# The affine step of a layer norm moved from ScalarE to VectorE in a transformer layer on eight cores

## The chip, the cores and the metric

The kernel runs on the 8 cores of one Trainium2 chip. All cores run the same program, each on its own 1024 tokens. The metric is the device time of the slowest core in microseconds. TensorE is called PE here, VectorE DVE, ScalarE ACT, GpSimd POOL and SyncE SP, as the profile calls them.

## What is computed

One layer: a gated linear attention with its own layer norm, a residual and a layer norm, a gated feed-forward network of inner width 8192, again a residual and a layer norm. Inputs are 4 x 2048 tokens of width 2048 in f32. The part that the change touches is the layer norm on `y`, its gate, and the product with `Wo` that follows:

```python
q = (x @ Wq).reshape(B, S, H, Dh)
v = (x @ Wv).reshape(B, S, H, Dh)
# states: new = sigmoid(beta) * prev + v_t, along the tokens
y = (q * states).reshape(B, S, D)
mu = jnp.mean(y, axis=-1, keepdims=True)
var = jnp.var(y, axis=-1, keepdims=True)
y = (y - mu) * jax.lax.rsqrt(var + LN_EPS) * ln_g + ln_b
gate = jax.nn.silu(x @ Wg)
y = y * gate
return y @ Wo
...
x = _layernorm(x + attention(x))
h = jax.nn.silu(x @ w_gate.T) * (x @ w_up.T)
x = _layernorm(x + h @ w_down.T)
```

## The kernel before, in words

The program is written by hand for each engine: every block (`@blk.vector`, `@blk.scalar`, ...) appends its instructions to the queue of one engine, in the order of the Python code, and engines wait for each other on counting semaphores. `tick` lets an instruction raise its engine's semaphore (sT, sV, sS, sP for PE, DVE, ACT, POOL) and returns the count; `mil` keeps such counts by name, and `wait_ge(sX, n)` holds an engine's queue until engine X has reached n. An engine also waits for itself in this way, where one of its instructions reads what the one before it has written: `v.wait_ge(sV, cnt["V"])`. Nothing reorders the queues.

Stages, in order: load and transpose x (`tbuf`, features in partitions, 16 tiles of 128 x 1024 tokens); q projection into `qbuf`; carry-in state; v projection into `vbuf`; scan over 8 chunks of tokens with the gate projection between the chunks, its Silu going to `bbuf`; sums for the layer norm on `y` (L698 squares on DVE, L710 and L714 column sums on PE); the row statistics on one partition (L734 to L756); a broadcast of them over 128 partitions by PE into four PSUM banks (L764, L765): `p[n2]` holds 1/std and `p[2+n2]` holds -mu/std of the 512 tokens of half n2.

Then comes the loop around the change (L774 to L816). It runs over n2 (two halves of 512 tokens) and over the 16 feature tiles dt, 32 turns in all. A turn takes one 128x512 tile of `qbuf` and does, on DVE, `tmp = y * p[n2]` (L790) and `tmp = tmp + p[2+n2]` (L793); on ACT, `tmp2 = Identity(tmp * ln_g + ln_b)` with both as per-partition operands from `lngb` (L801); on DVE, `y = tmp2 * gate` (L811), bf16, back into `qbuf`. `tmp` and `tmp2` are f32 views of the two halves of the bf16 scratch tile `sqscr`. There is one `tmp` and one `tmp2`, so turns don't overlap, but for the first instruction of a turn, which may start as soon as ACT is done with the turn before.

The `Wo` product follows (L958 to L1006): for each half of the `wo` panels, each of 8 chunks of 128 tokens and each of 4 panels, PE accumulates 16 matmuls over the feature tiles (L981) in bank 4 or 5 in turn. Each of the 16 waits for its tile's turn of the loop (`mil[("y2", gk)]`, L980). The bank is freed by a cast on DVE (L995). All casts stand in DVE's queue behind all 32 turns. The `wo` panels come by DMA from POOL's queue (L266, from L956 and L964), and SP loads x for the residual (L831). After that DVE and ACT do the layer norm (L841 to L902), PE transposes (L927), and the feed-forward network runs in 64 pairs of gate and up products (L1090, L1121) with the down product (L1184) between them.

Of the kernel before, what the change touches and what calls it, by code (L numbers as in the profile page):

```python
# [7 lines left out]
F32 = mybir.dt.float32  # L8
BF16 = mybir.dt.bfloat16
AF = mybir.ActivationFunctionType  # L10
ALU = mybir.AluOpType
# [27 lines left out]
def build_program(c: Cfg):  # L39
    nc = bass.Bass("TRN2", target_bir_lowering=False)  # L40
    D, TOK, INTER = c.D, c.TOK, c.INTER
    H, KT, NCH, NT, NN2 = c.H, c.KT, c.NCH, c.NT, c.NN2
# [33 lines left out]
    qbuf = sbuf("qbuf", [128, KT * TOK], BF16)  # L76
# [15 lines left out]
    lngb = sbuf("lngb", [128, 2 * KT], F32)  # L92
# [5 lines left out]
    sqscr = sbuf("sqscr", [128, max(2 * TOK, D, 4 * NT)], BF16)  # L98
# [6 lines left out]
    p = [psum(f"p{i}", [128, 512], F32) for i in range(7)]  # L105
# [7 lines left out]
    sT, sV, sS, sP = sem("sT"), sem("sV"), sem("sS"), sem("sP")  # L113
    cnt = {"T": 0, "V": 0, "S": 0, "P": 0}
    semmap = {"T": sT, "V": sV, "S": sS, "P": sP}

    def tick(inst, e, k=1):
        inst.then_inc(semmap[e], k)
        cnt[e] += k
        return cnt[e]  # L120
# [6 lines left out]
    def dtick(inst, name):  # L127
        ds[name][1] += 16
        inst.then_inc(ds[name][0], 16)
        return (name, ds[name][1])  # L130
# [17 lines left out]
    blk = es.enter_context(nc.Block())  # L148
    mil = {}
# [16 lines left out]
    @blk.sync  # L166
    def _(sy):
        dtick(sy.dma_start(llrow[:1, :H], beta16), "small")
        dtick(sy.dma_start(llrow[:1, H:H + 1], cflag), "small")
        dtick(sy.dma_start(lngb[:, 0:KT], lng_col), "small")  # L170
        mil["small_in"] = dtick(sy.dma_start(lngb[:, KT:2 * KT], lnb_col),
                                "small")
# [176 lines left out]
    for pi in range(NPAN):  # L349
# [6 lines left out]
        for dtl in range(NDT):  # L356
            dt = pi * NDT + dtl
# [412 lines left out]
    mil["l1bc_done"] = cnt["T"]  # L770

    first_y2 = [True]
    prev_y2 = [None]
    for n2 in range(NN2):  # L774
        for pi in range(NPAN):
            for dtl in range(NDT):
                dt = pi * NDT + dtl
                ggrp = pi * NDT * NN2 + dtl * NN2 + n2

                @blk.vector  # L780
                def _(v, dt=dt, n2=n2, ggrp=ggrp):
                    if first_y2[0]:
                        first_y2[0] = False
                        v.wait_ge(sT, mil["l1bc_done"])
                    v.wait_ge(sS, mil[("gsil", ggrp)])
                    if prev_y2[0] is not None:
                        v.wait_ge(sS, mil[("y2t3", prev_y2[0])])
                    ysl = qbuf[:, dt * TOK + n2 * NT: dt * TOK + (n2 + 1) * NT]
                    tmp = sqscr[:, 0:2 * NT].bitcast(F32)
                    tick(v.tensor_mul(tmp, ysl, p[n2][:, 0:NT]), "V")  # L790
                    v.wait_ge(sV, cnt["V"])
                    mil[("y2t2", ggrp)] = tick(
                        v.tensor_add(tmp, tmp, p[2 + n2][:, 0:NT]), "V")  # L793

                @blk.scalar
                def _(sc, dt=dt, n2=n2, ggrp=ggrp):
                    sc.wait_ge(sV, mil[("y2t2", ggrp)])
                    tmp = sqscr[:, 0:2 * NT].bitcast(F32)
                    tmp2 = sqscr[:, 2 * NT:4 * NT].bitcast(F32)
                    mil[("y2t3", ggrp)] = tick(  # L800
                        sc.activation(tmp2, tmp, AF.Identity,  # L801
                                      bias=lngb[:, KT + dt:KT + dt + 1],
                                      scale=lngb[:, dt:dt + 1]), "S")

                @blk.vector
                def _(v, dt=dt, n2=n2, ggrp=ggrp):
                    v.wait_ge(sS, mil[("y2t3", ggrp)])
                    ysl = qbuf[:, dt * TOK + n2 * NT: dt * TOK + (n2 + 1) * NT]
                    tmp2 = sqscr[:, 2 * NT:4 * NT].bitcast(F32)
                    gsl = bbuf[:, dt * TOK + n2 * NT: dt * TOK + (n2 + 1) * NT]  # L810
                    inst = v.tensor_mul(ysl, tmp2, gsl)  # L811
                    mil[("y2", ggrp)] = tick(inst, "V")
                prev_y2[0] = ggrp
                if n2 == NN2 - 1:
                    mil[("y2dt", dt)] = cnt["V"]
        mil[("y2h", n2)] = cnt["V"]  # L816
# [490 lines left out]
def _get_nc(cfg):  # L1307
    key = (cfg.D, cfg.TOK, cfg.INTER, cfg.WINP)
    if key not in _NC_CACHE:
        _NC_CACHE[key] = build_program(cfg)  # L1310
    return _NC_CACHE[key]
# [66 lines left out]
```

## Time and profile before

| | |
|---|---|
| runs shown | 2313.89 and 2378.39 us, median 2346.14 us |
| profiled execution, its own time | 2313.54 us |
| its span, slowest core (core 5) | 2311.9 us |
| spans of the eight cores | 2302.1 to 2311.9 us |
| PE busy | 1921.7 us, 83% of the span |
| DVE busy | 557.8 us, 24% |
| ACT busy | 410.1 us, 18% |
| POOL busy | 110.2 us, 5% |

The profiled execution is one run, and its span is the time from the first to the last instruction of the slowest core. A busy time is the sum over the whole span. A low share says nothing about a stage: an engine can be idle for most of the span and still be what others wait for in one stage of it. Rows are read with start times in us from the start of the span, and a bracket at the end of a row gives the idle time of the engine before that instruction and who ended it.

### The profile page before, as it was taken

What the parts mean: (1) busy time and instruction counts of PE and PEld (TensorE: products, weight loads), DVE (VectorE), ACT (ScalarE), POOL (GpSimd) and SP (SyncE); (2) the same over time, 40 slices, a digit from 0 to 9 for tenths busy, and PEclk for the clock granted to TensorE, in tenths of its full rate; (3) what the DMA queues carried; (4) which work ended last, traced back from release to release, by engine and by line L of the source; (5) the groups of instructions that cost most, each with busy time, mean ns of one, the idle gap of its engine ahead of it and who ended that gap; (6) DMA issues with size and microseconds to landing.
All of it is one profiled execution on the core that took longest, in us unless ns stands there. A gap on an engine that the chain in (4) does not pass through costs nothing.

```text
span 2311.9 us, 25430 instructions; the slowest of 8 cores (2302.1 to 2311.9 us)
## 1 busy us (share of the span) xinstructions
PE 1921.7 (83%) x9898; PEld 970.9 (42%) x9898; DVE 557.8 (24%) x1319; ACT 410.1 (18%) x466; POOL 110.2 (5%) x230
## 2 busy tenths in 40 slices
PE   4898999811196639999999999999999999997760
PEld 2347864300164424444444444444444444443320
DVE  4222234644413450010111101111111111111154
ACT  0100015334300102222121121121112112110002
POOL 1000000000000000000000000000000000000000
PEclk9999999955597759999999999999999999999885
DMA  8652343420005105335453354353444334423113
GB/s 122 115 91 37 58 72 72 71 59 0 0 11 104 70 2 90 73 73 96 86 92 73 55 94 84 57 95 73 74 73 91 74 55 91 77 43 64 37 37 145
DMA packets 32452, 161.03 MB, mean 70 GB/s; under 512 B 3668, under 2 KB 3668, under 8 KB 22100
## 3 DMA queue, kind: packets, MB, share of 16 engines
q0 software_dynamic: 29744, 142.62, 34.6%
q1 hardware_dynamic: 2596, 16.79, 1.9%
q8 instruction: 85, 1.39, 0.2%
q14 instruction: 27, 0.22, 0.0%
HBM read 293.62 MB, written 8.39 MB: 131 GB/s over the span
## 4 chain that ended last, share of the span: by engine, by line
PE 78%; DVE 8%; DMA 5%; ACT 5%; issue 4%; DVEq 0%; POOL 0%; ACTq 0%; POOLq 0%; SPq 0%
PE p L1090 19%; PE p L1121 19%; PE p L1184 18%; PE p L981 5%; PE p L492 5%; PE p L590 5%; PE p L370 4%; DMA warena<-wd_t 2%; ACT L801 2%; DMA bbuf<-x_loc 1%; ACT sqscr L801 1%; DVE sqscr L793 1%; DVE sqscr L790 1%; DMA warena<-wo 1%; DVE mscr L1025 1%
## 5 line engine op out<-in xcount | busy, mean ns | idle before, releaser
L1090 PE MATMUL p<-tbuf,warena 128*128 128x512 bf16 x2048 | 465.0, 380 | 7.4 <-DMA warena<-wgu_t 7.4
L1121 PE MATMUL p<-tbuf,warena 128*128 128x512 bf16 x2048 | 462.9, 379 | 0.0
L1108 ACT ACT_TABLE_LOAD x128 | 164.2, 1283 | 1015.5 <-PE p L1090 1015.5
L1090 PEld LDWEIGHTS p<-tbuf,warena 128*128 128x128 bf16 x2048 | 200.8, 98 | 250.6 <-issue 10.4
L981 PE MATMUL p<-warena,qbuf 128*128 128x256 bf16 x1024 | 155.1, 304 | 177.8 <-DVE bbuf L995 101.1
L1121 PEld LDWEIGHTS p<-tbuf,warena 128*128 128x128 bf16 x2048 | 200.3, 98 | 241.7
L1184 PE MATMUL p<-warena,vbuf 128*128 128x512 bf16 x1024 | 232.1, 389 | 42.0 <-DMA warena<-wd_t 34.2
L1184 PE MATMUL p<-warena,qbuf 128*128 128x512 bf16 x1024 | 222.3, 379 | 0.0
L981 PEld LDWEIGHTS p<-warena,qbuf 128*128 128x128 bf16 x1024 | 109.6, 107 | 224.6 <-issue 188.1
L1200 DVE TENSOR_TENSOR bbuf<-bbuf,p 128x512 bf16<-128x512 bf16 x128 | 88.0, 687 | 378.9 <-PE p L1184 378.9
L1184 PEld LDWEIGHTS p<-warena,vbuf 128*128 128x128 bf16 x1024 | 101.2, 100 | 172.3 <-issue 58.4
L1184 PEld LDWEIGHTS p<-warena,qbuf 128*128 128x128 bf16 x1024 | 100.2, 98 | 120.8
L1141 DVE TENSOR_TENSOR qbuf<-sscr,p 128x512 bf16<-128x512 f32 x64 | 44.0, 688 | 407.6 <-PE p L1121 407.6
L1141 DVE TENSOR_TENSOR vbuf<-sscr,p 128x512 bf16<-128x512 f32 x64 | 44.0, 688 | 398.2 <-PE p L1121 398.2
L370 PE MATMUL p<-tbuf,warena 128*128 128x512 bf16 x512 | 114.5, 388 | 10.6 <-DVE qbuf L384 8.5
L590 PE MATMUL p<-tbuf,warena 128*128 128x512 bf16 x512 | 114.8, 383 | 0.0
L1050 POOL DMA_DIRECT2D warena<-wgu_t x128 | 67.6, 533 | 970.0 <-PE p L1121 798.0
L492 PE MATMUL p<-warena,tbuf 128*128 128x256 bf16 x1024 | 113.5, 273 | 0.0
L492 PEld LDWEIGHTS p<-warena,tbuf 128*128 128x128 bf16 x1024 | 99.7, 98 | 13.5 <-issue 2.0
L606 ACT ACT_TABLE_LOAD x32 | 41.1, 1283 | 311.6 <-PE p L590 311.6
L370 PEld LDWEIGHTS p<-tbuf,warena 128*128 128x128 bf16 x512 | 50.9, 100 | 73.9 <-issue 16.2
L1108 ACT ACTIVATE sscr<-p 128x512 f32<-128x512 f32 x128 | 76.4, 597 | 1.4
(126 smaller groups left out, 780.9 us busy)
## 6 DMA issues: line engine op xcount, KB each, us to landing
warena<-wgu_t POOLq DMA_DIRECT2D x128, 512.0 KB, 6.9
warena<-wd_t POOLq DMA_DIRECT2D x32, 1024.0 KB, 13.3
warena<-wq POOLq DMA_DIRECT2D x8, 1024.0 KB, 9.4
warena<-wv POOLq DMA_DIRECT2D x8, 1024.0 KB, 9.9
warena<-wg POOLq DMA_DIRECT2D x8, 1024.0 KB, 8.9
warena<-wo POOLq DMA_DIRECT2D x8, 1024.0 KB, 18.5
sscr<-x_loc SPq DMA_DIRECT2D x8, 1024.0 KB, 4.8
out_loc<-sscr SPq DMA_DIRECT2D x8, 1024.0 KB, 4.1
```

What stands on the lines that cost most here:

```text
L370: inst = t.matmul(p[bk][:, 0:NT], warena[:, slot * WSL + k * PW + dtl * 128: slot * WSL + k * PW + (dtl + 1) * 128], tbuf[:, k * TOK + n2 ...
L492: inst = t.matmul(p[bk][:, 0:PW], tbuf[:, k * TOK + ci * 128: k * TOK + (ci + 1) * 128], warena[:, slot * WSL + k * PW: slot * WSL + (k + ...
L590: inst = t.matmul(p[bk][:, 0:NT], warena[:, slot * WSL + k * PW + dtl * 128: slot * WSL + k * PW + (dtl + 1) * 128], tbuf[:, k * TOK + n2 ...
L801: sc.activation(tmp2, tmp, AF.Identity, bias=lngb[:, KT + dt:KT + dt + 1], scale=lngb[:, dt:dt + 1]), "S")
L981: inst = t.matmul(p[bk][:, 0:PW], qbuf[:, k * TOK + ci * 128: k * TOK + (ci + 1) * 128], warena[:, pl * WSL + k * PW: pl * WSL + (k + 1) * ...
L1050: return dtick(g.dma_start(AP(warena, slot * GUSL, [[WARENA, 128], [1, GUSL]]), AP(wgu_t.tensor, pj * 128 * GUSL, [[GUSL, 128], [1, GUSL]] ...
L1090: inst = t.matmul(p[gbk][:, 0:NT], warena[:, (j % 2) * GUSL + k * OPW + ot * 128: (j % 2) * GUSL + k * OPW + (ot + 1) * 128], tbuf[:, k * ...
L1108: inst = sc.activation(sscr[:, SIL_OFF + (gg % 2) * NT: SIL_OFF + (gg % 2 + 1) * NT], p[gbk][:, 0:NT], AF.Silu)
L1121: inst = t.matmul(p[ubk][:, 0:NT], warena[:, (2 + j % 2) * GUSL + k * OPW + ot * 128: (2 + j % 2) * GUSL + k * OPW + (ot + 1) * 128], tbuf ...
L1141: inst = v.tensor_mul(buf[:, off + ot * TOK + n2 * NT: off + ot * TOK + (n2 + 1) * NT], sscr[:, SIL_OFF + (gg % 2) * NT: SIL_OFF + (gg % 2 ...
L1184: inst = t.matmul(p[bk][:, 0:512], buf[:, off + ot * TOK + ci * 128: off + ot * TOK + (ci + 1) * 128], warena[:, WD_OFF + sub * WDSL + klo ...
L1200: inst = v.tensor_add(asl, asl, p[bk][:, 0:512])
```

## The change

In each of the 32 turns the multiply-add with `ln_g` and `ln_b` is no longer done by ACT (`activation` with Identity) but by DVE (`tensor_scalar` with mult and add, both operands again per partition from `lngb`), in place on `tmp`. The second scratch view `tmp2` is not used any more. The waits between DVE and ACT within a turn are gone. In their place each of the four DVE instructions of a turn waits for the DVE instruction ahead of it, the first one of a turn too, where it waited for ACT's last result before.

```diff
--- before.py
+++ after.py
@@ -770,7 +770,6 @@
     mil["l1bc_done"] = cnt["T"]
 
     first_y2 = [True]
-    prev_y2 = [None]
     for n2 in range(NN2):
         for pi in range(NPAN):
             for dtl in range(NDT):
@@ -783,34 +782,20 @@
                         first_y2[0] = False
                         v.wait_ge(sT, mil["l1bc_done"])
                     v.wait_ge(sS, mil[("gsil", ggrp)])
-                    if prev_y2[0] is not None:
-                        v.wait_ge(sS, mil[("y2t3", prev_y2[0])])
+                    v.wait_ge(sV, cnt["V"])
                     ysl = qbuf[:, dt * TOK + n2 * NT: dt * TOK + (n2 + 1) * NT]
                     tmp = sqscr[:, 0:2 * NT].bitcast(F32)
                     tick(v.tensor_mul(tmp, ysl, p[n2][:, 0:NT]), "V")
                     v.wait_ge(sV, cnt["V"])
-                    mil[("y2t2", ggrp)] = tick(
-                        v.tensor_add(tmp, tmp, p[2 + n2][:, 0:NT]), "V")
-
-                @blk.scalar
-                def _(sc, dt=dt, n2=n2, ggrp=ggrp):
-                    sc.wait_ge(sV, mil[("y2t2", ggrp)])
-                    tmp = sqscr[:, 0:2 * NT].bitcast(F32)
-                    tmp2 = sqscr[:, 2 * NT:4 * NT].bitcast(F32)
-                    mil[("y2t3", ggrp)] = tick(
-                        sc.activation(tmp2, tmp, AF.Identity,
-                                      bias=lngb[:, KT + dt:KT + dt + 1],
-                                      scale=lngb[:, dt:dt + 1]), "S")
-
-                @blk.vector
-                def _(v, dt=dt, n2=n2, ggrp=ggrp):
-                    v.wait_ge(sS, mil[("y2t3", ggrp)])
-                    ysl = qbuf[:, dt * TOK + n2 * NT: dt * TOK + (n2 + 1) * NT]
-                    tmp2 = sqscr[:, 2 * NT:4 * NT].bitcast(F32)
+                    tick(v.tensor_add(tmp, tmp, p[2 + n2][:, 0:NT]), "V")
+                    v.wait_ge(sV, cnt["V"])
+                    tick(v.tensor_scalar(tmp, tmp, lngb[:, dt:dt + 1],
+                                         lngb[:, KT + dt:KT + dt + 1],
+                                         ALU.mult, ALU.add), "V")
+                    v.wait_ge(sV, cnt["V"])
                     gsl = bbuf[:, dt * TOK + n2 * NT: dt * TOK + (n2 + 1) * NT]
-                    inst = v.tensor_mul(ysl, tmp2, gsl)
+                    inst = v.tensor_mul(ysl, tmp, gsl)
                     mil[("y2", ggrp)] = tick(inst, "V")
-                prev_y2[0] = ggrp
                 if n2 == NN2 - 1:
                     mil[("y2dt", dt)] = cnt["V"]
         mil[("y2h", n2)] = cnt["V"]
```

On DVE, at the head of the loop, right behind the statistics. Before (the branches are the borders of the program's blocks; sT, sV, sS are the semaphores of PE, DVE and ACT):

```order
L756 SCALAR_TENSOR_TENSOR sscr<-sscr 1x512 [waits sV]
L780 UNCONDITIONAL_BRANCH
L790 TENSOR_TENSOR sqscr<-qbuf,p 128x512 [waits sT,sS]
L793 TENSOR_TENSOR sqscr<-sqscr,p 128x512 [waits sV]
L805 UNCONDITIONAL_BRANCH
L811 TENSOR_TENSOR qbuf<-sqscr,bbuf 128x512 [waits sS]
L780 UNCONDITIONAL_BRANCH
L790 TENSOR_TENSOR sqscr<-qbuf,p 128x512 [waits sS]
```

And now, with line numbers of the changed kernel:

```order
L756 SCALAR_TENSOR_TENSOR sscr<-sscr 1x512 [waits sV]
L779 UNCONDITIONAL_BRANCH
L788 TENSOR_TENSOR sqscr<-qbuf,p 128x512 [waits sT,sS,sV]
L790 TENSOR_TENSOR sqscr<-sqscr,p 128x512 [waits sV]
L792 TENSOR_SCALAR sqscr<-sqscr,lngb 128x512 [waits sV]
L797 TENSOR_TENSOR qbuf<-sqscr,bbuf 128x512 [waits sV]
L779 UNCONDITIONAL_BRANCH
L788 TENSOR_TENSOR sqscr<-qbuf,p 128x512 [waits sS,sV]
```

A turn has four DVE instructions instead of three, all of them with a wait on DVE's own semaphore; the last one no longer waits on ACT. The block border within the turn is gone. The order of everything else on DVE is as before.

On ACT, at the end of the loop, before:

```order
L801 ACTIVATE sqscr<-sqscr,lngb 128x512 [waits sV]
L795 UNCONDITIONAL_BRANCH
L801 ACTIVATE sqscr<-sqscr,lngb 128x512 [waits sV]
L874 UNCONDITIONAL_BRANCH
L878 ACTIVATE mscr<-mscr,epsc 128x1 [waits sV]
```

And now the rows that follow the statistics (L748) directly:

```order
L748 ACTIVATE sscr<-sscr,epsc 1x512 [waits sV]
L744 UNCONDITIONAL_BRANCH
L748 ACTIVATE sscr<-sscr,epsc 1x512 [waits sV]
L859 UNCONDITIONAL_BRANCH
L863 ACTIVATE mscr<-mscr,epsc 128x1 [waits sV]
```

The 32 ACT instructions are gone, and the Sqrt of the second layer norm (L878 before, L863 now) stands right behind the Sqrt of the first. PE, POOL and SP keep their instructions and their order.

## Rows read from the trace of the kernel before

**Rows 1.** Span and mean granted clock by core.

```profile
core 3: 2302.1 us, clock 0.914
...
core 5: 2311.9 us, clock 0.916
```

**Rows 2.** The page: busy tenths in 40 slices of 57.8 us, and the chain's lines.

```profile
PE   4898999811196639999999999999999999997760
...
PEclk9999999955597759999999999999999999999885
...
PE p L1090 19%; PE p L1121 19%; PE p L1184 18%; PE p L981 5%; PE p L492 5%; PE p L590 5%; PE p L370 4%; DMA warena<-wd_t 2%; ACT L801 2%; DMA bbuf<-x_loc 1%; ACT sqscr L801 1%; DVE sqscr L793 1%; DVE sqscr L790 1%; DMA warena<-wo 1%; DVE mscr L1025 1%
```

**Rows 3.** Windows: us, busy us (instructions) by engine, PE clock, DMA share, GB/s.

```profile
490.00:556.00 66.00, 5.57 (x15) 1.56 (x15) 29.76 (x46) 31.43 (x30) 0.00 (x0) 0.50 0.06 24
556.00:627.00 71.00, 3.91 (x18) 2.36 (x18) 32.71 (x51) 33.53 (x32) 0.00 (x0) 0.52 0.00 0
486.00:627.00 141.00, 9.48 (x33) 3.92 (x33) 63.98 (x98) 67.06 (x64) 0.00 (x0) 0.51 0.04 15
...
1000.00:2000.00 1000.00, 1000.00 (x4634) 453.32 (x4633) 129.98 (x189) 189.88 (x202) 65.51 (x124) 1.00 0.43 78
```

**Rows 4.** Timeline, first turns and last: start us, us, engine, line, operation [idle before].

```profile
486.10 0.69 DVE L790 TENSOR_TENSOR sqscr<-qbuf,p 128x512 f32<-128x512 bf16 x1 [4.32 <-PE p L765]
...
490.48 0.68 DVE L790 TENSOR_TENSOR sqscr<-qbuf,p 128x512 f32<-128x512 bf16 x1
...
491.26 0.69 DVE L793 TENSOR_TENSOR sqscr<-sqscr,p 128x512 f32<-128x512 f32 x1
492.03 1.28 ACT L801 ACT_TABLE_LOAD   x1 [2.26 <-DVE sqscr L793]
493.32 0.81 ACT L801 ACTIVATE sqscr<-sqscr,lngb 128x512 f32<-128x512 f32 x1
494.24 0.69 DVE L811 TENSOR_TENSOR qbuf<-sqscr,bbuf 128x512 bf16<-128x512 f32 x1 [2.29 <-ACT sqscr L801]
494.85 0.68 DVE L790 TENSOR_TENSOR sqscr<-qbuf,p 128x512 f32<-128x512 bf16 x1
...
556.62 0.37 PE L981 MATMUL p<-warena,qbuf 128*128 128x256 bf16 x1 [4.35 <-DVE qbuf L811]
...
625.72 0.69 DVE L811 TENSOR_TENSOR qbuf<-sqscr,bbuf 128x512 bf16<-128x512 f32 x1 [2.29 <-ACT sqscr L801]
```

**Rows 5.** Groups by line in 486 to 627 us: busy us, mean ns, idle before.

```profile
L801 ACT ACT_TABLE_LOAD x32 | 41.1, 1283 | 80.6 <-DVE sqscr L793 80.6
L801 ACT ACTIVATE sqscr<-sqscr,lngb 128x512 f32<-128x512 f32 x32 | 26.0, 812 | 0.4
...
L793 DVE TENSOR_TENSOR sqscr<-sqscr,p 128x512 f32<-128x512 f32 x32 | 22.0, 688 | 3.3
...
L981 PE MATMUL p<-warena,qbuf 128*128 128x256 bf16 x33 | 9.8, 392 | 131.6 <-DVE bbuf L995 66.5 <-DVE qbuf L811 65.1
```

**Rows 6.** Groups of DVE by line over the whole span, shapes kept apart.

```profile
L841 DVE SCALAR_TENSOR_TENSOR bbuf<-bbuf,sscr 128x2048 bf16<-128x2048 bf16 x8 | 18.3, 2293 | 0.8
...
L1280 DVE TENSOR_SCALAR sscr<-bbuf,mscr 128x2048 f32<-128x2048 bf16 x8 | 10.7, 1346 | 10.3 <-DMA out_loc<-sscr 10.3
...
L753 DVE RECIPROCAL sscr<-sscr 1x512 f32<-1x512 f32 x2 | 6.7, 3340 | 4.4 <-ACT sscr L748 4.4
L902 DVE TENSOR_SCALAR bbuf<-bbuf,mscr 128x2048 bf16<-128x2048 bf16 x8 | 6.4, 803 | 0.0
```

**Rows 7.** Line 286 (tensor_scalar, f32): duration ns min/median/max.

```profile
L286 DVE TENSOR_SCALAR sscr<-tscr,llbc x16: 270/274/661, 47.3 to 53.4; 128x128 f32<-128x128 f32 x16
```

**Rows 8.** Timeline of the GpSimd queue, 400 to 700 us.

```profile
441.35 2.12 POOL L266 DMA_DIRECT2D warena<-wo  x4 [28.89 <-PE p L590]
687.79 0.54 POOL L266 DMA_DIRECT2D warena<-wo  x1 [244.33 <-PE p L981]
```

**Rows 9.** Timeline of ACT behind the stage.

```profile
737.20 1.28 ACT L878 ACT_TABLE_LOAD   x1 [111.58 <-DVE mscr L871]
```

## The prediction

> **What bounds the kernel now.** I read the cores first [rows 1]: the slowest and the fastest lie 10 us apart and hold nearly the same mean granted clock, so one core may stand for all. Then the page's slices and its chain of waits [rows 2]: TensorE (PE) is nearly full everywhere but in one hole around slices 8 to 11, and its clock digit falls to 5 there. The chain gives the lines of the changed loop (L790, L793, L801, L811) their shares of the end-to-end path, so this hole is not beside the critical path, it is the path. The windows [rows 3] give it borders: in 486 to 627 us PE is busy for 9.5 of 141 us, VectorE (DVE) for 64 and ScalarE (ACT) for 67. DVE and ACT together are 131 of 141 us and neither is more than half full: they take turns.
>
> The timeline [rows 4] shows one turn. In order of starts: L790 at 490.48, L793 at 491.26, ACT's table load at 492.03, ACT's multiply-add at 493.32, L811 at 494.24, the next L790 at 494.85. The steps are 0.78, 0.77, 1.29, 0.92 and 0.61 us, together 4.37 us. It happens 32 times. The stage runs from the first L790 (486.10) to the end of the last L811 (625.72 + 0.69 = 626.41): 140.3 us. Who waits for it? PE needs all 16 results of the first half before its first group is complete (that group starts in full at 556.62), then fills its two banks and stands for 66 us [rows 5], because the casts that free the banks (L995) are queued on DVE behind all 32 turns [rows 4, 5]. The whole stage is thus exposed, both halves.
>
> **The change part by part.** (1) ACT's part goes: 32 table loads of 1.283 us and 32 multiply-adds of 0.812 us [rows 5], with both hand-overs. That is the 0.77 + 1.29 + 0.92 us of a turn, less what DVE needs anyway. (2) A fourth DVE instruction comes, a tensor_scalar over 128x512 f32, in place, with two per-partition operands. (3) Two waits on DVE's own semaphore come with it, and a third at the head of each turn where the wait on ACT stood. Behind each of them in DVE's queue stand only the rest of the turns and then the casts for which PE waits, so all of it counts.
>
> A wait of DVE on itself can be read: L790 takes 0.68 and L793 starts 0.78 after it [rows 4]. So it costs 0.10 us from end to start. The new turn is:
> - multiply to add: 0.78
> - add to tensor_scalar: 0.69 + 0.10 = 0.79
> - tensor_scalar to last multiply: T + 0.10
> - last multiply to the next turn: 0.69 + 0.10 = 0.79. Before it was 0.61, since the next L790 was let in while L811 was still finishing; the new wait at the turn's head ends that overlap and costs 0.18 x 32 = 5.8 us of the gain.
>
> Sum: 2.46 + T, and for the stage 32 x (2.46 + T) - 0.10.
>
> T is not in the trace, so it is bounded by the nearest rows [rows 6]. The two rows that also carry two per-partition operands are L902, 128x2048 bf16 to bf16, 0.803 us, and L1280, 128x2048 bf16 to f32, 1.346 us. If L1280 streams at half the speed of L902, the streaming part of L1280 is 2 x (1.346 - 0.803) = 1.086 us and 0.26 us are fixed. That is 0.53 ns per element. The tensor_tensor rows grow from 0.688 us at 512 elements to 2.293 us at 2048 (L793 [rows 5] and L841 [rows 6]), which is 1.045 ns per element: so L1280 does run at double that rate. At L1280's rate 512 elements take 0.27, and T = 0.27 + 0.26 = 0.53 us. From above: the plain rate is 0.688 us for 512 elements, as L793 has it, and with the fixed 0.26 of the two-operand rows 0.535 + 0.26 = 0.80 us. From below: L286 does f32 to f32 with one per-partition operand in 0.274 us [rows 7] for a quarter of the elements, and more elements can't take less, so T is over 0.27. I take 0.53, since L1280 has the same operand form and the same output type.
>
> The stage then takes 32 x 2.99 - 0.10 = 95.6 us, and 140.3 - 95.6 = 44.7 us go.
>
> What could eat that? PE's input weights are no obstacle: the four wo panels are issued at 441 us [rows 8] and the transfers are over soon after 490 (share 0.06 over 490 to 556, and 0.00 in 556 to 627 [rows 3]). ACT's next work, the Sqrt of L878, comes at 737 us and has a table load ahead of it already [rows 9]. The GpSimd queue issues nothing between 441 and 688 [rows 8]. Edits that cost nothing: the dropped `prev_y2` wait and the unused half of `sqscr`. PE's clock stands at half in the hole (0.50 to 0.52 [rows 3]) and in the first us after it; a hole of 96 us still leaves it there, so its climb from 627 on is only moved. The second half of PE's wait shrinks from 66 us to about 45, and the first half's turns too.
>
> **One rule weighed against the rows.** L1280 and L286 show double rate for tensor_scalar between SBUF tiles, and 0.26 us fixed with two operands. The Trainium skill (VectorE: DVE Perf Modes, section "The perf-mode tier table (the rule you actually need)") says that tensor_scalar on fp32 in SBUF gets 2x, where tensor_tensor on fp32 stays at 1x, and gives 1227 ns for 2048 elements. The trace agrees on the rate, but its L1280 row is 0.12 us longer than the page's figure for the same count. An estimate from the page's figure alone, less 1536 elements at 0.53 ns, would be T = 0.41 us and a time of 2265.1 us.
>
> **The sum** is made against the profiled execution: 2313.5 us, of which the span is 2311.9. 2313.5 - 44.7 = 2268.8 us, 1.9% less. The median of the two runs shown is 2346.1 (2313.9 and 2378.4), so the profiled execution stands 32.6 us below it, beside the lower run. My number goes by the profiled execution; a median over such a pair would lie some 30 us higher, and I let the upper end of the range take in most of that.
>
> **The rivals.**
> - A shorter T. If the fixed part is that of the one-operand row, 0.274 - 128 x 0.53 ns = 0.21 us, T = 0.48, the stage takes 94.0 us, 46.3 us go and the time is 2267.2. This lies on the edge of 2%, and each 0.01 us less in T is 0.3 us more of gain. The page's rule named above leans this way. For it: L286 is f32 to f32 as the new one is. Against it: both two-operand rows want 0.26. Chance 0.30, with what else might add a few us.
> - Plain rate. T = 0.69 to 0.80 us, if an in-place f32 instruction is not paired as L1280 is. 39.6 to 36.1 us go: 2273.9 to 2277.4. Against it: L286 and L1280. Chance 0.06.
> - Something else ends the hole: the change does what it says on DVE but PE gets its data no earlier, as it waits for a panel or for a bank. Then up to all of the gain is lost, 2313.5 us. Against it: [rows 3, 5, 8], where no transfer runs in the hole's second half and PE's two waits are for DVE alone. Chance 0.02.
> - Slower: the new instruction is a slow kind, as there are [rows 6]. L753 (RECIPROCAL, f32, 512 elements) takes 3.34 us against the 0.69 of L793. With T = 3.34 the stage takes 185.5 us, 45.2 more than before, 2358.7 us. It turns slower from T = 1.93 on, and by over 2% from 3.37. Every tensor_scalar row in the trace speaks against it. Chance 0.01, and another 0.02 for a lower granted clock in the long stretch of matmuls behind the change, of which 1000 to 2000 us is shown with 1.00 granted [rows 3]: to end 2% slower it would have to lose the 44.7 us gained and 46.3 more, a clock of 0.92 over those 1000 us.
>
> **How the numbers follow.** 2% of 2313.5 is 46.3 us, about what a measurement of this kernel can tell from no change; my forecast of 44.7 lies just inside. Forecast (T from 0.49 to 0.60) 0.59, shorter T 0.30, plain rate 0.06, other cover 0.02, slower 0.03. Faster by over 2%: the shorter T, and a little of the forecast, whose error of 1.6 us is all that parts it from the limit: 0.35. Within 2%: 0.62. Slower: 0.03. The low end, 2261, is T near 0.27; the high end, 2300, takes in the plain rate (2277) and most of the 32.6 us by which the median of before lies above its profiled execution.
>
> **What would show it right or wrong.** In the profile after: 32 rows of a tensor_scalar of 0.53 us each (0.48 to 0.60); turns of 2.99 us from one L788 to the next; the first L788 still near 486 and the last L797 ending near 582; no ACT work in the stage; PE's wait for the casts down from 66 to about 45 us; PE busy 500 of 500 us later on, with a clock of 1.00. It is wrong if the tensor_scalar takes 0.69 or more, if the turn is longer than its four parts, or if the 44.7 us saved by the stage are not found again in the span.

## The result, and the profile after

The changed kernel takes 2272.8 us (median of 11 runs) against 2314.1 us for the kernel before (median of 10 runs, among them new ones beside it). The ratio is 0.9824 with a 95% interval of 0.9813 to 0.9835: shorter by 1.8%, 41.3 us. That is clear of the scatter, but less than the 2% from which on the forecast calls a kernel faster. The profiled execution took 2272.6 us, its slowest core is core 3 now. The forecast was 2268.8 us. In some executions the cores of one or both dies show a lower granted clock and the time is longer, up to 2626.7 us for the changed kernel, and the medians count these while the ratios and the profiles do not.

The cores of the changed kernel, first and last in span, answer to [rows 1]:

```profile
core 3: 2270.9 us, clock 0.925
core 4: 2256.4 us, clock 0.925
```

The page's slices and chain, which answer to [rows 2] (a slice is 56.8 us now):

```profile
PE   4898999931676469999999999999999999997750
...
PEclk9999999965788769999999999999999999999885
...
PE p L1075 20%; PE p L1106 19%; PE p L1169 18%; PE p L492 5%; PE p L590 5%; PE p L966 5%; PE p L370 4%; DMA warena<-wd_t 2%; DMA bbuf<-x_loc 2%; DVE sqscr L788 1%; DVE sqscr L790 1%; DMA warena<-wo 1%; DVE qbuf L797 1%; DVE mscr L1010 1%; DVE sqscr L792 1%
```

The hole in PE's row starts at the same slice and is shorter by about one. ACT is gone from the list of lines, and all four DVE lines of a turn stand there with 1% each, where it had L790 and L793 before.

The windows, which answer to [rows 3] (columns: us, busy us and instructions of PE, PEld, DVE, ACT and POOL, PE clock, DMA share, GB/s):

```profile
486.00:586.00 100.00, 11.34 (x35) 4.20 (x33) 83.82 (x129) 0.00 (x0) 0.00 (x0) 0.50 0.05 21
...
1000.00:2000.00 1000.00, 1000.00 (x4635) 453.38 (x4634) 130.01 (x189) 189.88 (x202) 65.52 (x124) 1.00 0.44 79
```

DVE is busy for 84 of the 100 us of the stage, ACT for none. What is left of DVE's time are the hand-overs between its own instructions, so DVE alone sets the length of the stage now. The granted clock in it is 0.50, as before, and 1.00 in the long stretch of matmuls.

The timeline of the first turn of core 3 and of the last, which answers to [rows 4] (start us, us, engine, line, operation):

```profile
488.09 0.69 DVE L788 TENSOR_TENSOR sqscr<-qbuf,p 128x512 f32<-128x512 bf16 x1 [4.35 <-PE p L765]
488.88 0.69 DVE L790 TENSOR_TENSOR sqscr<-sqscr,p 128x512 f32<-128x512 f32 x1
489.68 0.55 DVE L792 TENSOR_SCALAR sqscr<-sqscr,lngb 128x512 f32<-128x512 f32 x1
490.33 0.69 DVE L797 TENSOR_TENSOR qbuf<-sqscr,bbuf 128x512 bf16<-128x512 f32 x1
491.13 0.69 DVE L788 TENSOR_TENSOR sqscr<-qbuf,p 128x512 f32<-128x512 bf16 x1
...
585.10 0.69 DVE L797 TENSOR_TENSOR qbuf<-sqscr,bbuf 128x512 bf16<-128x512 f32 x1
585.71 0.75 DVE L980 CAST bbuf<-p 128x256 bf16<-128x256 f32 x2
```

The steps are 0.79, 0.80, 0.65 and 0.80 us: a turn of 3.04 us, where it was 4.37. The stage runs from 488.09 to 585.10 + 0.69 = 585.79, 97.7 us, where it was 140.3.

Groups in the stage, and behind them PE's waits, which answer to [rows 5]:

```profile
L797 DVE TENSOR_TENSOR qbuf<-sqscr,bbuf 128x512 bf16<-128x512 f32 x32 | 22.1, 692 | 3.3
L788 DVE TENSOR_TENSOR sqscr<-qbuf,p 128x512 f32<-128x512 bf16 x32 | 22.0, 688 | 7.9 <-PE p L765 4.3 <-DVE qbuf L797 0.5
L790 DVE TENSOR_TENSOR sqscr<-sqscr,p 128x512 f32<-128x512 f32 x32 | 22.0, 687 | 3.7 <-DVE sqscr L788 0.5
L792 DVE TENSOR_SCALAR sqscr<-sqscr,lngb 128x512 f32<-128x512 f32 x32 | 17.5, 546 | 3.5
```

```profile
PE p L966 <- DVE bbuf L980: 45.4, 1, 45.4
PE p L966 <- DVE qbuf L797: 43.6, 16, 3.3
```

PE's wait for the bank (L980, the casts) fell from 66.5 to 45.4 us and its waits for the first half's turns from 65.1 to 43.6. The rows of L788 and L790 also show 0.5 us each of idle time on DVE itself: two hand-overs of the stage, at the same two instructions on all eight cores, take about 0.46 us and not 0.11. The kernel before has one such. What makes them long is not shown.

Where the time went can be read core by core. For each core I took the start of the first turn, the end of the last, and the span; the means over the eight cores, in us, here with all kernels run for this study:

| kernel | first turn starts | stage | from its end to the span's end | span |
|---|---|---|---|---|
| before | 485.3 | 140.3 | 1681.0 | 2306.6 |
| changed | 485.5 | 97.7 | 1680.5 | 2263.7 |
| e1, ACT in one block | 492.7 | 100.7 | 1681.9 | 2275.2 |
| e2, two steps | 486.4 | 114.0 | 1681.5 | 2281.9 |
| e3, three fused | 485.1 | 81.8 | 1680.8 | 2247.7 |
| e4, ACT beside DVE | 486.1 | 75.5 | 1680.7 | 2242.3 |
| e5, two tiles | 485.4 | 91.7 | 1686.7 | 2263.8 |
| e6, casts between turns | 486.2 | 102.2 | 1654.2 | 2242.6 |
| e7, fused pairs | 485.8 | 63.4 | 1683.8 | 2233.0 |
| e8, fused and casts | 485.6 | 80.6 | 1651.8 | 2218.1 |
| e9, fused pairs and casts | 485.3 | 69.6 | 1648.0 | 2202.9 |

The change took 42.6 us out of the stage and left what is before and behind it as it was. All of it came through to the mean span (42.9 us).

The stage is the same to 0.2 us on all eight cores of a kernel. What lies before and behind it is not: in the profiled executions of e1, e5, e6 and e7 two neighbouring cores are late by 10 to 27 us, before the stage in e1 (cores 4 and 5, whose first turn starts at 510 and 513 us), behind it in e5 and e6 (cores 2 and 3) and e7 (cores 0 and 1). Their cause is not shown, and it blurs the spans and times of these four. The column of the stage is the sure one.

### The profile page after: what moved, and what is told of

Same layout as the page of the kernel before. It is cut to its first block, busy times and chain, and to the rows that moved or that the text cites. A ratio compares the mean times of both kernels' runs of the same rounds, so it can differ in the third digit from the quotient of the medians.

```text
span 2270.9 us, 25399 instructions; the slowest of 8 cores (2256.4 to 2270.9 us)
## 1 busy us (share of the span) xinstructions
PE 1917.2 (84%) x9898; PEld 969.9 (43%) x9898; DVE 578.3 (25%) x1351; ACT 343.0 (15%) x402; POOL 110.2 (5%) x230
## 4 chain that ended last, share of the span: by engine, by line
PE 79%; DVE 10%; DMA 5%; issue 3%; ACT 2%; DVEq 0%; POOL 0%; ACTq 0%; POOLq 0%; SPq 0%
PE p L1075 20%; PE p L1106 19%; PE p L1169 18%; PE p L492 5%; PE p L590 5%; PE p L966 5%; PE p L370 4%; DMA warena<-wd_t 2%; DMA bbuf<-x_loc 2%; DVE sqscr L788 1%; DVE sqscr L790 1%; DMA warena<-wo 1%; DVE qbuf L797 1%; DVE mscr L1010 1%; DVE sqscr L792 1%
## 5 line engine op out<-in xcount | busy, mean ns | idle before, releaser
L1093 ACT ACT_TABLE_LOAD x128 | 164.2, 1283 | 1015.3 <-PE p L1075 1015.3
L1169 PEld LDWEIGHTS p<-warena,vbuf 128*128 128x128 bf16 x1024 | 100.7, 99 | 172.9 <-issue 57.9
L606 ACT ACT_TABLE_LOAD x32 | 41.1, 1283 | 313.5 <-PE p L590 313.5
## 6 DMA issues: line engine op xcount, KB each, us to landing
warena<-wo POOLq DMA_DIRECT2D x8, 1024.0 KB, 18.4
```

The costliest lines, as they stand in the source:

```text
L606: inst = sc.activation(bbuf[:, dt * TOK + n2 * NT: dt * TOK + (n2 + 1) * NT], p[bk][:, 0:NT], AF.Silu)
L1093: inst = sc.activation(sscr[:, SIL_OFF + (gg % 2) * NT: SIL_OFF + (gg % 2 + 1) * NT], p[gbk][:, 0:NT], AF.Silu)
L1169: inst = t.matmul(p[bk][:, 0:512], buf[:, off + ot * TOK + ci * 128: off + ot * TOK + (ci + 1) * 128], warena[:, WD_OFF + sub * WDSL + klo ...
```

## The experiments

**e1: the old arithmetic, one block for ACT.** In the kernel before each of ACT's 32 multiply-adds is written as a block of its own, and each has a table load ahead of it. Here they stand in one block, in the same queue order and with the same waits.

```diff
-                @blk.scalar
-                def _(sc, dt=dt, n2=n2, ggrp=ggrp):
-                    sc.wait_ge(sV, mil[("y2t2", ggrp)])
...
-                    mil[("y2t3", ggrp)] = tick(
-                        sc.activation(tmp2, tmp, AF.Identity,
...
+                cnt["S"] += 1
+                mil[("y2t3", ggrp)] = cnt["S"]
+                y2act.append((dt, mil[("y2t2", ggrp)]))
...
+    @blk.scalar
+    def _(sc):
...
+        for dt, need in y2act:
+            sc.wait_ge(sV, need)
+            sc.activation(tmp2, tmp, AF.Identity,
+                          bias=lngb[:, KT + dt:KT + dt + 1],
+                          scale=lngb[:, dt:dt + 1]).then_inc(sS, 1)
```

> The kernel of before, with the 32 multiply-adds of ACT written in one block of the program. Theory 1 (the change won the time of the table loads, and a load stands ahead of every ACT instruction only because each opens a block of its own): one table load instead of 32, the turn falls from 4.37 to 3.08 us, the kernel to about 2273 us, as far as the change went, with ACT still doing the multiply-add. Rival (the load belongs to the change of function, or the gain is that of leaving ACT): 32 loads, turn 4.37 us, 2314 us.

Its timeline of ACT, at the loop's start (core 5, which reaches the stage later than most):

```profile
514.12 1.28 ACT L820 ACT_TABLE_LOAD   x1 [10.06 <-DVE sqscr L794]
515.41 0.81 ACT L820 ACTIVATE sqscr<-sqscr,lngb 128x512 f32<-128x512 f32 x1
518.51 0.81 ACT L820 ACTIVATE sqscr<-sqscr,lngb 128x512 f32<-128x512 f32 x1 [2.28 <-DVE sqscr L794]
521.60 0.81 ACT L820 ACTIVATE sqscr<-sqscr,lngb 128x512 f32<-128x512 f32 x1 [2.28 <-DVE sqscr L794]
```

One load instead of 32, and turns of 3.09 us (518.51 to 521.60). The stage takes 100.7 us. The kernel's time is inconclusive: the median of four runs is 2288.2 us, the two shortest took 2276.3 and 2276.9 us, and the ratio to the kernel before is 0.987, interval 0.9798 to 0.9941. For the stage theory 1 holds: the repeated loads were 39.6 of the 42.6 us that the change took from it, and this could be had without moving the arithmetic. Moving it to DVE is worth the last 3 us of the stage. The Trainium skill (ScalarE: Activation LUTs, section "What ACT_TABLE_LOAD costs") gives about 1283 ns for the load and about 1380 ns more for a drain, 2.66 us for every switch to a different set of functions. The rows here agree with the first figure. The second is not seen: the turn fell by 1.28 us, the load alone. But all 32 turns use one function, and whether a switch between sets would show a drain, these runs don't tell.

**e2: the new instruction in two steps.** A multiply and an add, each with one per-partition operand.

```diff
-                    tick(v.tensor_scalar(tmp, tmp, lngb[:, dt:dt + 1],
-                                         lngb[:, KT + dt:KT + dt + 1],
-                                         ALU.mult, ALU.add), "V")
+                    tick(v.tensor_scalar_mul(tmp, tmp, lngb[:, dt:dt + 1]),
+                         "V")
+                    v.wait_ge(sV, cnt["V"])
+                    tick(v.tensor_scalar_add(tmp, tmp,
+                                             lngb[:, KT + dt:KT + dt + 1]),
+                         "V")
```

> The changed kernel, with the tensor_scalar split in two, a multiply and an add with one per-partition operand each. Theory 1 (the stage is exposed one for one): each takes 0.48 us (0.21 fixed and 0.27 streamed) with 0.10 to the next, the turn grows from 3.035 to 3.55 us and the kernel by 16 us, to 2289. Rival (the stage is only partly on the path, as 41 us came of 43): the kernel grows by less than the stage does, by under 12 us.

Its groups of the stage:

```profile
L792 DVE TENSOR_SCALAR sqscr<-sqscr,lngb 128x512 f32<-128x512 f32 x32 | 15.6, 486 | 3.4
L795 DVE TENSOR_SCALAR sqscr<-sqscr,lngb 128x512 f32<-128x512 f32 x32 | 15.6, 486 | 3.4
```

The stage grew by 16.3 us and the kernel to 2287.7 us, 14.9 more than the changed one (ratio to before 0.9884, 0.9864 to 0.9903). That is theory 1. The form with one operand and one operation takes 0.486 us, the form with two of each 0.546: the second pair costs 0.06 us.

**e3: three instructions in place of four.** (y g) r + (m g), then (+ b) times the gate, as three scalar_tensor_tensor.

```diff
-                    tick(v.tensor_mul(tmp, ysl, p[n2][:, 0:NT]), "V")
+                    gcol = lngb[:, dt:dt + 1]
+                    bcol = lngb[:, KT + dt:KT + dt + 1]
+                    tick(v.scalar_tensor_tensor(tmp, ysl, gcol, p[n2][:, 0:NT],
+                                                ALU.mult, ALU.mult), "V")
                     v.wait_ge(sV, cnt["V"])
-                    tick(v.tensor_add(tmp, tmp, p[2 + n2][:, 0:NT]), "V")
-                    v.wait_ge(sV, cnt["V"])
-                    tick(v.tensor_scalar(tmp, tmp, lngb[:, dt:dt + 1],
-                                         lngb[:, KT + dt:KT + dt + 1],
-                                         ALU.mult, ALU.add), "V")
+                    tick(v.scalar_tensor_tensor(tmp, p[2 + n2][:, 0:NT], gcol,
+                                                tmp, ALU.mult, ALU.add), "V")
                     v.wait_ge(sV, cnt["V"])
...
-                    inst = v.tensor_mul(ysl, tmp, gsl)
+                    inst = v.scalar_tensor_tensor(ysl, tmp, bcol, gsl,
+                                                  ALU.add, ALU.mult)
```

> The changed kernel, with the four DVE instructions of a turn folded into three scalar_tensor_tensor. Theory 1: three instructions of 0.69 to 0.74 us with 0.10 us each, a turn of 2.37 to 2.52 us, the stage 16 to 21 us shorter than the changed kernel's and the kernel at 2252 to 2257 us. Rival (scalar_tensor_tensor with a per-partition operand and a PSUM input is slower than that, from 0.91 us on): no gain over the changed kernel, 2273 us.

Its timeline of DVE over one turn:

```profile
500.33 0.75 DVE L790 SCALAR_TENSOR_TENSOR sqscr<-qbuf,lngb,p 128x512 f32<-128x512 bf16 x1
501.19 0.75 DVE L793 SCALAR_TENSOR_TENSOR sqscr<-p,lngb,sqscr 128x512 f32<-128x512 f32 x1
502.04 0.75 DVE L797 SCALAR_TENSOR_TENSOR qbuf<-sqscr,lngb,bbuf 128x512 bf16<-128x512 f32 x1
502.89 0.75 DVE L790 SCALAR_TENSOR_TENSOR sqscr<-qbuf,lngb,p 128x512 f32<-128x512 bf16 x1
```

An instruction takes 0.75 us, 0.06 more than the plain tensor_tensor, and the turn 2.56 us (500.33 to 502.89). Both are a little over what was expected (0.69 to 0.74 and 2.37 to 2.52). The stage is 15.9 us shorter than the changed kernel's and the time 2256.1 us, ratio 0.9743 (0.9724 to 0.9762).

Is it the operand or the second operation that costs the 0.06 us? The row statistics ahead of the stage have a scalar_tensor_tensor on f32 with two operations and a constant in place of the per-partition operand (L756), beside a plain tensor_tensor of the same size (L738). In the changed kernel:

```profile
L738 DVE TENSOR_TENSOR sscr<-sscr 1x512 f32<-1x512 f32 x2 | 1.4, 680 | 0.2
L756 DVE SCALAR_TENSOR_TENSOR sscr<-sscr 1x512 f32<-1x512 f32 x2 | 1.4, 680 | 0.2
```

They take the same time, on one partition. So in the two-tensor form the second operation is free and the operand is what costs. For tensor_scalar no run parts the two.

**e4: ACT kept with all its loads, but working beside DVE.** Two scratch tiles, and the last multiply of a turn behind the first two of the next.

```diff
-                    if prev_y2[0] is not None:
-                        v.wait_ge(sS, mil[("y2t3", prev_y2[0])])
+                    if turn >= 2:
+                        v.wait_ge(sV, y2q[turn - 2])
...
-                    tmp = sqscr[:, 0:2 * NT].bitcast(F32)
+                    o = (turn % 2) * 2 * NT
+                    tmp = sqscr[:, o:o + 2 * NT].bitcast(F32)
...
+                if pend_y2[0] is not None:
+                    pend_y2[0]()
+                pend_y2[0] = finish
```

> The kernel of before, table loads kept, with two scratch tiles and DVE's last multiply put behind the next turn's first two instructions, so that ACT works beside DVE. Theory 1 (what cost was that the engines took turns, not ACT's work): the turn is bounded by DVE's three instructions or ACT's 1.28 + 0.81 with hand-over, 2.3 to 2.5 us, the kernel at 2248 to 2255 us, faster than the change. Rival (ACT's share has to leave): the turn stays above 3.0 us and the kernel at 2273 or more.

Its groups of the stage:

```profile
L805 ACT ACT_TABLE_LOAD x32 | 41.1, 1283 | 15.7 <-DVE sqscr L797 14.5
L805 ACT ACTIVATE sqscr<-sqscr,lngb 128x512 f32<-128x512 f32 x32 | 26.0, 813 | 0.4
L817 DVE TENSOR_TENSOR qbuf<-sqscr,bbuf 128x512 bf16<-128x512 f32 x32 | 22.1, 691 | 3.9 <-ACT sqscr L805 2.4
```

The 32 loads and 32 multiply-adds are all there, 67 us of ACT, and DVE's wait for ACT ahead of the last multiply is down from 73.6 us to 2.4. The stage takes 75.5 us, less than with the change. The ratio is 0.9728 (0.9705 to 0.9752); it rests on two of the four runs, at 2250.0 and 2253.0 us. So ACT's work, loads and all, cost time only because DVE stood still for it: the price was that ACT and DVE took turns. Three rows of ACT also bear on the drain of e1:

```profile
499.50 0.81 ACT L805 ACTIVATE sqscr<-sqscr,lngb 128x512 f32<-128x512 f32 x1
500.39 1.28 ACT L805 ACT_TABLE_LOAD   x1
501.69 0.81 ACT L805 ACTIVATE sqscr<-sqscr,lngb 128x512 f32<-128x512 f32 x1
```

The load starts 0.08 us behind the multiply-add ahead of it and the next multiply-add 0.02 us behind the load. Between neither pair is there room for 1.38 us.

**e5: a second scratch tile for the changed kernel.**

```diff
-                    v.wait_ge(sV, cnt["V"])
+                    turn = n2 * NPAN * NDT + dt
+                    if turn >= 2:
+                        v.wait_ge(sV, y2q[turn - 2])
+                    o = (turn % 2) * 2 * NT
...
-                    tmp = sqscr[:, 0:2 * NT].bitcast(F32)
+                    tmp = sqscr[:, o:o + 2 * NT].bitcast(F32)
...
+                    y2q[turn] = cnt["V"]
```

> The changed kernel with two scratch tiles used in turn, so that a turn's first instruction waits for the turn before last and no longer for the one just issued. Theory 1 (the wait at the turn's head costs 0.18 us, as the sum had it): 0.61 us from one turn's last multiply to the next turn's first, turn 2.85 us instead of 3.035, the stage 5.9 us shorter, the kernel at 2267 us. Rival (the spacing of 0.79 is DVE's own and not the wait's): turn 3.03 us, 2273 us.

Its timeline of DVE at the border of two turns:

```profile
502.58 0.69 DVE L801 TENSOR_TENSOR qbuf<-sqscr,bbuf 128x512 bf16<-128x512 f32 x1
503.19 0.68 DVE L792 TENSOR_TENSOR sqscr<-qbuf,p 128x512 f32<-128x512 bf16 x1
```

The next turn's first instruction starts 0.61 us behind the last multiply (502.58 to 503.19), in the changed kernel 0.80. The stage is 6.0 us shorter, as forecast. The kernel's time is inconclusive: the median of five runs is 2292.6 us and the shortest 2268.0, near the 2267 expected; the ratio is 0.9851 with an interval of 0.9795 to 0.9906, which covers the changed kernel's. The mean span did not fall, since the part behind the stage was 6 us longer in this execution, over half of it on two cores. That the 6.0 us reach the kernel's time is thus not shown.

**e6: the casts between the turns.** The first 15 groups of the `Wo` product and their casts are put behind the turns of the second half, one behind each from the second on (`emit_o` holds what the loop at L943 to L987 of the changed kernel emits).

```diff
                 if n2 == NN2 - 1:
                     mil[("y2dt", dt)] = cnt["V"]
+                    if dt >= 1:
+                        emit_o(0, ogrp[0] // PH, ogrp[0] % PH)
```

> The changed kernel with the first 15 casts of the Wo product, and PE's groups for them, placed between the turns of the second half, one behind each turn from the second on. Theory 1 (the 45 us in which PE waits are owed to the casts' place in DVE's queue, behind all turns): the stage grows by 15 x 0.5 us, PE does 15 of its 64 groups inside it at some 2.2 us each, the kernel falls by 20 to 28 us below the changed one, to 2245 to 2253 us. Rival (PE at half clock takes 3.7 us for a group and holds up DVE's turns by as much as it wins): 2265 to 2280 us.

A part of its timeline of PE, and one turn of DVE from the same stretch:

```profile
534.75 3.57 PE L796 MATMUL p<-warena,qbuf 128*128 128x256 bf16 x16
541.11 6.30 PE L796 MATMUL p<-warena,qbuf 128*128 128x256 bf16 x32 [2.79 <-DVE bbuf L810]
547.85 2.18 PE L796 MATMUL p<-warena,qbuf 128*128 128x256 bf16 x16 [0.44 <-DVE bbuf L810]
551.22 2.17 PE L796 MATMUL p<-warena,qbuf 128*128 128x256 bf16 x16 [1.19 <-DVE bbuf L810]
```

```profile
546.58 0.69 DVE L844 TENSOR_TENSOR qbuf<-sqscr,bbuf 128x512 bf16<-128x512 f32 x1
547.18 0.42 DVE L810 CAST bbuf<-p 128x256 bf16<-128x256 f32 x1
547.71 0.69 DVE L835 TENSOR_TENSOR sqscr<-qbuf,p 128x512 f32<-128x512 bf16 x1
...
549.95 0.69 DVE L844 TENSOR_TENSOR qbuf<-sqscr,bbuf 128x512 bf16<-128x512 f32 x1
550.55 0.42 DVE L810 CAST bbuf<-p 128x256 bf16<-128x256 f32 x1
```

The turns grew by 0.34 us only, to 3.37, since the cast overlaps with the multiply ahead of it, and PE does a group in each. PE is at the slow clock for the first groups (3.57 us) and then takes 2.2 us. DVE does not wait for it. The stage grew by 4.5 us, what comes behind it shrank by 26.3 us, and the mean span fell by 21.1. Two of the 15 groups PE had finished inside the stage in the changed kernel too (by 540.9 us on core 3), with which its two banks were full; 13 are new there. A small part of the gain is the clock's: in the changed kernel the first 4.3 us of PE's work behind the stage (586.4 to 590.7) have a granted clock of 0.50, in e6 it is 1.00 there already. Half of that time, some 2 of the 26.3 us, is an estimate of its worth. The median is 2263.4 us, above the 2245 to 2253 expected, with two runs at 2255.0 and 2255.8; the ratio is 0.9762 (0.9740 to 0.9784). The gain in the span is as large as theory 1 wanted, the size of the gain in the time stays less sure: cores 2 and 3, of which core 3 is the slowest, took 12 to 15 us more behind the stage than the others.

**e7: fused and interleaved in pairs.** The steps of e3 for two tiles by turns, so that no instruction waits for the one just ahead.

```diff
+                for step in range(3):
+                    for dt, dtl, ggrp in pr:
+                        o = dtl * 2 * NT
+                        tmp = sqscr[:, o:o + 2 * NT].bitcast(F32)
...
+                            if y2prev[dtl] is not None:
+                                v.wait_ge(sV, y2prev[dtl])
...
+                            v.wait_ge(sV, st[dtl])
...
```

> The three-instruction turn of e3, with two turns interleaved step by step on two scratch tiles, so that no instruction waits for the one just ahead of it. Theory 1 (of each 0.85 us of e3, 0.10 is the wait on the instruction before and some 0.08 the missing overlap with it): 0.67 to 0.72 us from start to start, turn 2.0 to 2.15 us, the stage 13 to 17 us shorter than e3's, the kernel at 2238 to 2243 us. Rival (the instructions stand 0.85 us apart whatever they wait for): as e3, 2255 us.

Its timeline of DVE over one pair (a row with x2 holds both tiles of a step):

```profile
501.49 1.41 DVE L808 SCALAR_TENSOR_TENSOR qbuf<-sqscr,lngb,bbuf 128x512 bf16<-128x512 f32 x2
502.81 1.40 DVE L798 SCALAR_TENSOR_TENSOR sqscr<-qbuf,lngb,p 128x512 f32<-128x512 bf16 x2
504.13 1.40 DVE L803 SCALAR_TENSOR_TENSOR sqscr<-p,lngb,sqscr 128x512 f32<-128x512 f32 x2
505.45 0.74 DVE L808 SCALAR_TENSOR_TENSOR qbuf<-sqscr,lngb,bbuf 128x512 bf16<-128x512 f32 x1
```

A pair takes 3.96 us (501.49 to 505.45), 0.66 us for an instruction, and so a turn 1.98, where e3 had 2.56. The stage takes 63.4 us, 18.4 us less than in e3, where 13 to 17 were expected. The time is 2236.2 us, 2 us under the expected range, the ratio 0.9662 (0.9644 to 0.9679).

**e8: the fused turn, two tiles and the casts of e6.**

> The three-instruction turn, two scratch tiles in turn, and the casts between the turns as in e6. Theory 1 (the gains are of the same path and add up, until PE's groups of 2.2 to 3.7 us set the pace of the second half): the kernel at 2226 to 2239 us, the fastest of these. Rival (PE at half clock sets the pace and eats the casts' gain, since the turns are shorter than its groups): no better than the interleaved pairs, 2240 us or more.

Its edits are those of e3, e5 and e6 together, in short:

```diff
+                    if turn >= 2:
+                        v.wait_ge(sV, y2q[turn - 2])
+                    o = (turn % 2) * 2 * NT
...
+                    tick(v.scalar_tensor_tensor(tmp, ysl, gcol, p[n2][:, 0:NT],
+                                                ALU.mult, ALU.mult), "V")
...
+                    if dt >= 1:
+                        emit_o(0, ogrp[0] // PH, ogrp[0] % PH)
```

It took 2226.7 us, ratio 0.9611 (0.9594 to 0.9628), at the short end of what was expected. The gains add: e3's stage less the 6.0 us of e5 and plus the 4.5 us of e6 makes 80.3 us, and 80.6 were measured.

**e9: the pairs of e7 with the casts.** Two groups and casts behind each pair of the second half, 16 in all.

```diff
+            if n2 == NN2 - 1:
+                for dt, _d, _g in pr:
                     mil[("y2dt", dt)] = cnt["V"]
+                for _c in range(2):
+                    emit_o(0, ogrp[0] // PH, ogrp[0] % PH)
```

> The interleaved pairs of e7 and, behind each pair of the second half, two groups of the Wo product with their casts. Theory 1 (turn length and the casts' place are two separate costs of one path, so they add): against e8 the 32 turns are 0.39 us shorter each, 12.5 us, and one more group is moved, so 2210 to 2216 us, the fastest of all. Rival (with turns of 2 us PE's groups of 2.2 us and their half clock at the start set the pace of the second half): DVE waits for PE there and the time stays at 2220 us or more.

Its slices on the page (one is 55.2 us):

```profile
PE   4898999946866399999999999999999999997750
...
PEclk9999999977888599999999999999999999999985
```

It took 2212.1 us, ratio 0.9559 (0.9544 to 0.9574), faster than before by 4.4%, and inside what was expected. The 16 casts lengthened the stage by 6.2 us against e7, and DVE waited for PE for 0.8 us in all, so the rival is out. In the page's slices the hole in PE's row, three slices with a 1 before, is down to one with a 4.

## Why the prediction was right

**The bound.** That the stage lies on the path in both halves held. In the changed kernel and in e2 to e4, where nothing but the turns was changed, the mean span moves with the stage to within 2 us (before to changed -42.6 and -42.9; against the changed kernel e2 +16.3 and +18.2, e3 -15.9 and -16.0, e4 -22.2 and -21.4). In e7 it is -34.3 and -30.7. In e1 (+3.0 and +11.5) and e5 (-6.0 and +0.1) it does not show: there the late cores outside the stage hide so small a step. Of the lines that the prediction reads off the chain's list, L811 is not in it; L790, L793 and L801 are. And the row at 556.62 is the last matmul of PE's first group, not its start. Neither changes the argument.

**The sum.** Forecast 44.7 us, in the stage 42.6. The 2.1 us between them are in three terms. T was 0.546 for 0.53 us, which is 0.5 us over 32 turns. The other steps were 0.79 + 0.80 + 0.10 + 0.80 for 0.78 + 0.79 + 0.10 + 0.79: L788 takes 0.687 us when it doesn't start under the tail of the last multiply, not the 0.680 of L790 before, and each hand-over has 0.10 to 0.11. With the turn at 3.035 for 2.99 us that is 1.4 us together, and 32 turns would take 97.0 us. The last 0.7 us are the two long hand-overs, for which the sum had no term. Its starting point, the measured 140.3 us, held one such.

**From the stage to the kernel.** The slowest core gave 41.0 us (2311.9 to 2270.9) where the mean span gave 42.9. The slowest of eight is another core in each execution; core 3 came to the stage at 488.1, core 5 before at 486.1. The sum had no term for that, and the medians (41.3 us) show the same. Of the 4.0 us by which the time missed, 2.1 are thus the stage's and 1.6 this.

**T.** The bounds were 0.27 and 0.80, and the row it was taken from, L1280, was the right one: two per-partition operands at double rate. From L792 (0.546 us for 512 elements) to L1280 (1.346 for 2048) it is 0.52 ns per element, half the 1.045 of the two-tensor rows. The prediction also names L286 as showing double rate, which one length alone can't show; with e2's 0.486 us beside its 0.274 it does, 0.55 ns per element. L841, from which the plain rate was taken, is a scalar_tensor_tensor and no tensor_tensor, but one with a constant in place of the per-partition operand, so the rate stands. The rival with the shorter T borrowed the fixed part of a one-operand row; e2 shows its 0.48 to be right for one operand (0.486) and so not for two. The prediction's estimate from the Trainium skill (VectorE: DVE Perf Modes, section "The perf-mode tier table (the rule you actually need)"), 0.41 us, is too short by 0.13; two operands at about 0.06 us each would be nearly all of that. The double rate that the Trainium skill states there agrees with the 0.52 ns.

**The wait at the turn's head.** Costed at 0.18 us a turn, 5.8 us in all. e5 takes it away and the stage falls by 6.0 us.

**The other rivals.** Plain rate: out, 0.546 us. Something else ends the hole: out, as PE's wait ends with L797 and L980 as before. Slower: out; the clock in 1000 to 2000 us stayed at 1.00.

**What the argument had only in part.** The mechanism was right and no errors cancelled in the sum: every term that missed, missed toward a gain too large. But the argument took ACT's load, multiply-add and two hand-overs as one sum that leaves, which is right for the time. It didn't ask why a load stands ahead of each of 32 equal instructions, and e1 shows that 39.6 us of the gain in the stage lay there. Nor did it ask for the order of work: e4 gains more than the change with all of ACT's work kept.

## What to carry to other kernels

When two engines each show half of a stage as busy and a third waits for both, the price is in the taking of turns: try to overlap them with a second buffer before you move work from one to the other. Here the overlap alone gave a stage of 75.5 us and the move alone 97.7; the move gave less than that only with the arithmetic folded and interleaved (63.4). The overlap together with e1's single load was not tried. Look at what stands ahead of repeated instructions of ACT: equal functions in separate blocks each had their table load, and one block had one. And ask of an idle engine not only how long its producer takes but what the release of its buffer is queued behind; 15 casts moved between turns, with PE's groups for them, gave 21 us of mean span.

## What the runs showed of the hardware

A DVE instruction that waits for the one just ahead of it starts 0.10 us after its end, but for one or two hand-overs of a stage, with 0.46, and one that doesn't starts before that end: 0.61 us behind a 0.69 us multiply (e5), 0.66 us behind a 0.75 us one (e7). A per-partition operand adds about 0.06 us to a 128x512 instruction of the two-tensor form (0.688 us with none, 0.75 with one, and the second operation adds nothing by L738 and L756). For tensor_scalar the step from one operand and operation to two is as large (0.486 and 0.546 us). A table load of 1.283 us stood ahead of each of 32 equal ACT instructions written in 32 blocks, and once ahead of the same 32 written in one block (e1). The operand's price was not expected, as the rows before had no pair that differs in the operand alone.
